# Moving two of ten feed-forward steps from behind a recurrence to ahead of it in the second layer of a fused two-layer kernel

## What is computed

```
xn = layernorm(x);  x = x + latent_attention(xn) + mixture_0(xn)      # layer 0
xn = layernorm(x);  x = x + A(xn) + F(xn)                             # layer 1

A: z = zrms(xn); q,k,v,gate = z @ W_qkvz; short causal convolution, silu
   S_t = exp(g_t) S_(t-1) + k_t (beta_t (v_t - exp(g_t) k_t S_(t-1)))^T ; o_t = q_t S_t   # gated delta rule, 8 heads
   h = xn + (rms(o) * silu(gate)) @ W_out;  result h + mixture_1(zrms(h))
F: 8 dense experts, every token through each:
   out = sum over e of w_e(token) * (gelu(xn @ w1_e + b1_e) @ w2_e + b2_e), w_e nonzero for the top 2
```

## Time and profile before

| | us |
|---|---|
| median of 3 runs (2753.29 to 2766.41) | 2754.35 |
| the profiled execution: time | 2753.51 |
| the profiled execution: span | 2751.7 |
| from one pass's L1790 to the next one's, mean (first at 1231.9, eighth at 2711.7) | 211.4 |

### The profile page before, as it was taken

How to read it: one execution, slowest core, us unless ns; L and a number is a source line. 1 busy time by engine, 2 the same in 40 slices (tenths; PEclk the granted TensorE clock), 3 DMA queues, 4 the chain that set the end, 5 groups by cost and what they waited for, 6 DMA issues and landing times.

```text
span 2751.7 us, 48745 instructions
## 1 busy us (share of the span) xinstructions
PE 2447.3 (89%) x15408; PEld 1603.4 (58%) x15408; DVE 2025.2 (74%) x6361; ACT 1136.2 (41%) x2066; POOL 312.1 (11%) x236
## 2 busy tenths in 40 slices
PE   2989989898998987898899899899899899899898
PEld 1434444443444444686586586586586586577576
DVE  4858677685867667768768767867867867976976
ACT  0142232313232234446446446446445435545544
POOL 1000000000000002022021121110210211211211
PEclk9989989897988988998998998999999999999899
DMA  5230312213131221201201201201101101211211
GB/s 157 79 94 29 107 41 81 56 62 83 35 109 42 83 55 58 66 14 53 68 9 55 70 2 62 66 6 62 55 17 62 47 25 39 63 32 32 63 39 31
DMA packets 158271, 152.01 MB, mean 55 GB/s; under 512 B 81128, under 2 KB 122672, under 8 KB 157520
## 3 DMA queue, kind: packets, MB, share of 16 engines
q1 hardware_dynamic: 155024, 142.83, 18.0%
q10 hardware_dynamic: 3008, 6.36, 0.6%
HBM read 121.29 MB, written 27.85 MB: 54 GB/s over the span
## 4 chain that ended last, share of the span: by engine, by line
PE 57%; DVE 23%; issue 13%; ACT 3%; DMA 2%; POOL 1%; SPq 1%; DVEq 0%; ACTq 0%; POOLq 0%
PE bank L910 5%; PE bank L922 5%; PE bank L592 4%; PE bank L580 4%; PE bank L583 3%; PE bank L648 3%; DVE arena L1609 3%; PE bank L608 3%; PE bank L502 3%; DVE arena L1667 2%; DVE arena L1665 2%; PE bank L897 2%; DVE arena L1621 2%; PE bank L879 2%; PE bank L870 2%
## 5 line engine op out<-in xcount | busy, mean ns | idle before, releaser
L922 PEld LDWEIGHTS bank<-wring,arena 128*128 128x128 f32 x2048 | 275.6, 199 | 134.6 <-issue 97.3
L1168 ACT ACTIVATE arena<-bank,w_b 128x512 f32<-128x512 f32 x256 | 175.3, 687 | 363.6 <-PE bank L910 363.2
L910 PE MATMUL bank<-arena,wring 128*128 128x512 f32 x512 | 294.1, 661 | 28.7 <-ACT arena L1168 28.6
L922 PE MATMUL bank<-wring,arena 128*128 128x128 f32 x2048 | 281.1, 284 | 22.2 <-DVE arena L1782 15.2
L1609 DVE SCALAR_TENSOR_TENSOR arena<-bank,w_convw,arena 128x511 f32<-128x511 f32 (+2 forms) x384 | 255.0, 741 | 8.7 <-ACT arena L1078 8.5
L1047 ACT ACTIVATE arena<-bank 128x512 f32<-128x512 f32 (+1 forms) x384 | 172.7, 536 | 207.8 <-PE bank L635 206.3
L1453 DVE CUSTOM_DVE_ANT_0 bank<-bank,arena 128x128 f32<-128x128 f32 (+3 forms) x512 | 249.3, 493 | 0.0
L1034 ACT ACTIVATE arena<-bank 128x512 f32<-128x512 f32 x128 | 76.6, 598 | 405.0 <-PE bank L580 405.0
L502 PE MATMUL bank<-w_ident,arena 128*128 128x128 f32 (+2 forms) x652 | 111.6, 298 | 79.5 <-DVE arena L1349 34.1
L592 PE MATMUL bank<-arena 128*128 128x128 f32 x1088 | 163.7, 296 | 0.0
L592 PEld LDWEIGHTS bank<-arena 128*128 128x128 f32 x1088 | 137.7, 198 | 16.6 <-issue 8.9
(11 more groups left out here) (284 smaller groups left out, 4775.5 us busy)
## 6 DMA issues: line engine op xcount, KB each, us to landing
wring<-in_w_last SPq DMA_DIRECT2D x66, 512.0 KB, 3.3
arena<-scrw SPq DMA_DIRECT2D x260, 128.0 KB, 3.0
arena<-scrg SPq DMA_DIRECT2D x32, 512.0 KB, 5.4
arena<-scrq SPq DMA_DIRECT2D x36, 192.0 KB, 3.9
arena<-scrk SPq DMA_DIRECT2D x36, 192.0 KB, 4.5
scrn<-arena SPq DMA_DIRECT2D x64, 64.0 KB, 1.9
arena<-scrn SPq DMA_DIRECT2D x8, 512.0 KB, 3.7
scrx<-arena SPq DMA_DIRECT2D x8, 512.0 KB, 3.4
```

The source lines that it names most:

```text
L910: mm(bank[HBANK[f]][:, :], wring[:, e % 2, k * P:(k + 1) * P], xn1T, start=True, stop=True).then_inc(*s["p_fh"].up)
L922: last = mm(bank[o][:, t * P:(t + 1) * P], GH[:, f % 2, t * P:(t + 1) * P], wring[:, e % 2, FC * P + k * D:FC * P + (k + 1) * D], start=(f ...
L1168: fn(GH[:, f % 2, :], bank[HBANK[f]][:, :], ACT.Gelu_apprx_tanh, bias=W["b1"][:, f:f + 1]).then_inc(*s["a_gh"].up)
```

## The change

Steps 22 and 23 (fh, gelu, fo) leave the tail and stand behind step 21, ahead of `sz`, `tr` and `inv`. The sixth expert becomes one part (20, 24, bank 6), so there is one part fewer, and one `facc` fewer. The tail keeps eight steps: behind `swo` of chunk 2 come two of them ahead of `ct` of chunk 3 where there were three, one (as before) between `ct` and `swo` of chunk 3, and two ahead of `h2` where there were three. The other edits renumber waits.

```diff
-HBANK = (1,) + (7,) * 21 + (2,) * 10
-PARTS = ((0, 4, 6), (4, 8, 6), (8, 12, 2), (12, 16, 3), (16, 20, 6), (20, 22, 6), (22, 24, 3), (24, 28, 5), (28, 32, 3))
+HBANK = (1,) + (7,) * 23 + (2,) * 8
+PARTS = ((0, 4, 6), (4, 8, 6), (8, 12, 2), (12, 16, 3), (16, 20, 6), (20, 24, 6), (24, 28, 5), (28, 32, 3))
...
-    order += ffn(2) + ffn_rest() + [("sz", 2), ("sz", 3)]
+    order += ffn(4) + ffn_rest() + [("sz", 2), ("sz", 3)]
...
-    order += ffn(2) + [("nrm2", NT - 1, 0), ("nrm2", NT - 1, 1)] + ffn(1) + [("ct", NT - 1), ("facc", 6)] + ffn(1) + [("swo", NT - 1), ("h1",)] + ffn(3)
-    order += [("h2",), ("facc", 7), ("h3",)] + ffn(1) + [("h4",), ("gn",)] + ffn(2) + ffn_rest() + [("h5",), ("facc", 8), ("h5w",), ("gx",)]
+    order += ffn(1) + [("nrm2", NT - 1, 0), ("nrm2", NT - 1, 1)] + ffn(1) + [("ct", NT - 1)] + ffn(1) + [("swo", NT - 1), ("h1",)] + ffn(2)
+    order += [("h2",), ("facc", 6), ("h3",)] + ffn(1) + [("h4",), ("gn",)] + ffn(2) + ffn_rest() + [("h5",), ("facc", 7), ("h5w",), ("gx",)]
...
-                        need(*(("v_fo", 4), ("a_sz", 3), ("a_sz", 4), ("v_fo", 8), ("v_fo", 20), ("v_inv", INV_V * NT), ("v_o", 2 * NT),
-                               ("v_fo", 28))[part - 1])
+                        need(*(("v_fo", 4), ("a_sz", 3), ("a_sz", 4), ("v_fo", 8), ("v_fo", 20), ("v_o", 2 * NT),
+                               ("v_inv", INV_V * NT))[part - 1])
```

More of the change, by code:

```diff
@@ L846, in kt @@
                     if c < NT - 1:
-                        bk = after(*(("a_gh", 22), ("v_kd", 2), ("a_ct", 2))[c], 7)
+                        bk = after(*(("a_gh", 24), ("v_kd", 2), ("a_ct", 2))[c], 7)
                         for h in range(HK):
@@ L903, in ffn_hid @@
                         pe.wait_ge(*s["out_ready"].at(b, 0, late))
-                    elif f == 22:
+                    elif f == 24:
                         need("v_inv", INV_V * NT)
@@ L962, in moe1 @@
                     mm(bk[:, :], W["ge1"][:, p, :], hT, start=True, stop=True).then_inc(*s["p_gate1"].up)
-                    bk = after(*((("v_fo", 32), ("v_fo", 36))[p] if p < 2 else ("v_hid1", 2 * p - 3)), 5 - 2 * (p % 2))
+                    bk = after(*((("v_fo", 28), ("v_fo", 32))[p] if p < 2 else ("v_hid1", 2 * p - 3)), 5 - 2 * (p % 2))
                     mm(bk[:, :], W["ue1"][:, p, :], hT, start=True, stop=True).then_inc(*s["p_up1"].up)
@@ L1776, in accumulate @@
                     dve.wait_ge(*(s["v_fo"].at(b, 4 * n, late) if n else s["out_dma"].at(b, 0, late)))
-                    if n > 6:
+                    if n > 5:
                         dve.wait_ge(*s["v_mid"].at(b, 1, late))
@@ L1790, in h1 @@
                     link(v.tensor_tensor(x1[:, :, :], x1[:, :, :], zz, ALU.add))
-                    dve.wait_ge(*s["v_fo"].at(b, 28, late))
+                    dve.wait_ge(*s["v_fo"].at(b, 24, late))
                     v.tensor_tensor(facc, facc, x1[:, :, :], ALU.add).then_inc(*s["v_mid"].up)
```

## The result

The changed kernel takes 2807.64 us (median of 4, 2807.03 to 2809.54) beside 2757.76 for the one before (2753.29 to 2766.41): ratio 1.0178, 95% interval 1.0156 to 1.0199. It is 50 us slower. The forecast was slower, 2782, and its range ended at 2801: the sign was right, the size was not. The profiled execution took 2807.24, 53.7 more than that of before, which stands 4.3 under the median of its runs.

The account below looks back on a forecast made before the run. TensorE, busy 89%, was taken as the bound on average, but the last wait at each place counts. Losing 4.2 and gaining 0.75 a pass, 3.45 over 8 passes, adds 27.6 us: median 2782, range 2774 to 2790, with rivals 2767 to 2801.

Parts of the forecast that it names:

- T stays and the moved steps can't use the 1.13 ahead of fo 20: Ahead of the recurrence: fo 20's start T (1574.57 in pass 3) stays; new steps stand behind its 1.13 us wait.
- L1129 at T + 8.1, held by ScalarE's queue and not TensorE's: Ahead of the recurrence: silus behind gelu 23 end last; L1129 starts at 1582.7 in pass 3, not 1578.11.
- The table load costs what its row says: ScalarE ahead of the recurrence: load priced at the row's 1.28 us, without the further 1380 ns drain.
- 4.2 a pass lost, 0.75 gained: Each pass: recurrence starts 4.2 us later (mean of passes 3 and 8), tail becomes 0.75 us shorter.
- The sum: Whole kernel: net loss of 3.45 us a pass, 27.6 us over 8 passes; median 2782, 1.0% slower.
- The wait for ScalarE: Ahead of L795's second stage: TensorE idle for 0.5 to 1 us, listed as a sign of being right.
- the clock gets worse: Rival: more TensorE idle ahead of L1129, at ct and h2 lowers its clock; 18 us more, 2800; chance 0.16.
- The sign named for it: Recurrence: a clock row differing from pass to pass by more than the two edits do would show the forecast wrong.
- The waits at `ct` and `h2`: Tail: TensorE idle about 1 us at ct for L1762, and waiting at the transposes of h2 for L1799.
- The tail gives back both steps: Rival, tail: only TensorE counts, so 3.8 us a pass come back; 3 us lost, 2757; chance 0.08.
- only TensorE's queue counts: Rival, ahead of the recurrence: silus hidden, loss 3.2 us a pass, net 20 us, 2774; chance 0.08.
- the clock gets better: Rival: dense work just ahead of inv keeps the clock up; about 10 us come back, 2772; chance 0.10.

Follow-up runs that it names:

- bank2: Changed kernel with steps 16 to 19 accumulated in bank 2, so fo 20 needn't wait for the facc freeing bank 6: 2788.30 us (1.0104).
- copy_gates: Changed kernel with gates of chunks 2 and 3 copied, not put through silu, so no table load is needed there: 2780.66 us (1.0074).
- after_fill: Changed kernel with one needless 448-column matmul in TensorE's wait ahead of cv of chunk 0: 2791.21 us (1.0097).
- warm_after: Changed kernel with the needless matmuls of after_fill and of warm_before together: 2746.33 us (0.9953).
- warm_before: Kernel before the change with needless matmuls in two idle stretches of TensorE in the small mixture: 2738.63 us (0.9931).
- delay4: Kernel before the change with six VectorE memsets ahead of the transposes inv waits for, no step moved: 2833.05 us (1.0255).
- tail_alone: Kernel before the change with steps 22 and 23 left out altogether: 2760.99 us (0.9998).
- pad1: Changed kernel with two VectorE memsets added to each pass behind the last facc: 2812.21 us (1.0184).
- before_pad: Kernel before the change with five VectorE memsets added to each pass ahead of the last split of the weights: 2799.58 us (1.0138).
- one_step: Half of the change: only step 22 moved ahead of the recurrence, step 23 stays in the tail: 2787.31 us (1.0083).
- best1: one_step with steps 16 to 19 in bank 2 and the silu of chunks 2 and 3's gates done inside the recurrence: 2760.89 us (0.9999).

## Why the prediction was wrong

- *T stays and the moved steps can't use the 1.13 ahead of fo 20*: right. bank2 took that wait away, and L1129 came 0.78 earlier.
- *L1129 at T + 8.1, held by ScalarE's queue and not TensorE's*: right, 8.02 and 8.10 in the passes, and copy_gates shows TensorE's queue at 6.82, where T + 6.8 was worked out.
- *The table load costs what its row says*: right. The load took 1.28 and the silus began 0.01 behind it; the drain that the Trainium skill's page "ScalarE: Activation LUTs" adds in "What ACT_TABLE_LOAD costs" shows in no row here.
- *4.2 a pass lost, 0.75 gained*: 4.22 and 0.93. Pass by pass L1129 came 3.7 to 4.8 later, in pass 3 4.35 where 4.6 was worked out; that the mean of two passes comes so near to that of eight is partly luck. In the tail of pass 3 `swo` of chunk 3 came 0.13 earlier, as forecast, `h2` (L1799) 0.22 and not 0.1, and fh 29, fo 28 and `h4` behind it 0.9. The net was 26.4 us, not 27.6.
- *The sum* is the step that failed: it has no term for TensorE's clock and was made as if all else kept its time. The wait for ScalarE, which I named as 0.5 to 1 us of idle time and gave no price in the sum, stood ahead of a half clock through `inv` in six passes. By after_fill 15 us hang on it; beside before, which has falls there in four passes, L1129 to L860 and the recurrence are 11.1 us longer. Of the rest of the excess, 9.1 us are in the small mixture, 1.5 in the projections, and 5.6 ahead of the second loop, by which two profiles of that same code can differ. Half clock lasts 10.2 us in the mixture in seven passes of the changed kernel and 3.4 to 10.2 before. With the clock at 1.00 the mixture takes 19.64 (warm_after) and 19.46 (warm_before), so at full clock the moved steps make only 0.18 of its 1.14 a pass. Why the change made the fall there longer, beyond the new place of each pass, isn't shown.
- *The rival "the clock gets worse"* was the one that came true, with a chance of 0.16. It named one of the places, and a cause that after_fill bears out in part. Its price of 18 us was for the stretch from L795 to the third L897 alone, where 11.1 came, and it left out the mixture behind the tail; that its 2800 stands nearer to 2807.64 than the forecast is in part luck. The sign named for it, a granted clock that differs from pass to pass, didn't show: passes 2 to 7 fell alike, to 0.58 to 0.60 between L1129 and L860. The waits at `ct` and `h2`, which it named too, dropped nothing in the tail, which is at 1.00 in every pass. The Trainium skill's page "TensorE: Matmul & The Clock Gate", section "HAM oscillation — how this bites in real kernels", tells of a matmul kernel whose TensorE waits between bursts and starts each burst at half clock. The trace agrees for the long wait, since delay4 runs 10.1 us at 0.50 behind a wait of 4.40. For the wait of 0.78 it agrees only in part, since in six passes of bank2 the clock stays at 0.95 or more up to L860 behind the same wait.
- *The tail gives back both steps*, *only TensorE's queue counts*, *the clock gets better*: refuted by tail_alone, copy_gates and the windows. Two slips in the numbers didn't matter: the better clock's own terms (6.1, 1.2 and once more 6.1) make 13.4 and not 10, and with 2772 it lies above 2768, so "slower by over 0.5%" should have had some 0.9 and not 0.86.

What stays open: how much of the fall inside `inv` is due to its small products, and what decides in which passes it comes. Before the change it came in four of eight passes, with TensorE's idle times nearly the same in each. pad1 and before_pad shift the passes and leave the waits ahead of `inv` alone, and the falls there change in length and pass. So the place of a pass counts beside the wait, but by what rule no run shows.

## What to carry to other kernels

A chain of waits that shows one engine alone doesn't say that less work there shortens the path: ask when the next input is ready, from its own row; here 3.8 us of work taken out of such a chain gave 0.9. Before work is moved to a place where three engines arrive together, work out each queue to the instruction behind, the table load included. And a new idle time of TensorE may cost more than its own length, by the clock in what follows: fill it with needless matmuls into a free bank and look whether the granted clock stays up. Only the kernels with such filling in the small mixture came out faster than before, by 12 to 19 us. Where a kernel's clock falls at places that shift with every edit, compare each stretch over all passes, and the code that didn't change as well: here that alone differed by up to 9 us from one profile to another.

## What the runs showed of the hardware that was not expected

- A wait of TensorE of 0.78 us ahead of small matmuls was followed by 10.2 us at half clock in six of eight passes (after), and in two of eight with the same wait (bank2); with the wait filled by a needless matmul (1.02 us for its two records), L1129 to L860 took 6.6 us in six of eight passes, and 7.5 in the other two.
- Needless matmuls in waits of 0.84 and 2.17 us made the kernel 19 us faster (ratio 0.9931).
- Passes of a loop fell into equal lengths: 218.34 to 218.47 us for passes 2 to 7 of the changed kernel, 215.04 to 215.07 for passes 3 to 7 of bank2, 215.06 to 215.12 for passes 5 to 7 of one_step. The same lengths come again in kernels with other work: 218.40 and 218.43 for passes 6 and 7 of before_pad, 215.14 and 215.13 for passes 3 and 6 of best1.
- VectorE's 512-column memset takes 0.48 us, and one with a semaphore wait for itself every 0.66.
